# A Mamba and mixture-of-experts layer on one core: opening and first two units rewritten

## The reference, in short

```
dt = softplus(x_dbl[..., :R] @ dt_w.T + dt_b)
dA = exp(dt_t[..., None] * A);  h = h * dA + (dt_t * u_t)[..., None] * B_t[:, None, :]
y  = einsum('bdn,bn->bd', h, C_t) + u * Dp
```

## Time and profile before

| what | us |
|---|---|
| median of 3 runs | 554.12 (553.49 to 556.9) |
| profiled execution, its own time | 556.38 |
| its span, first to last instruction | 554.6 |

### The profile page before, as it was taken

One profiled execution on the slowest core, in us unless ns is written; L12 is line 12 of the kernel. 1 busy time (PEld: TensorE's weight loads), 2 busy tenths in 40 slices (PEclk: granted clock), 3 DMA queues, 4 the chain that ended last, 5 costly groups with the idle time before them and its releaser, 6 DMA issues.

```text
span 554.6 us, 5648 instructions
## 1 busy us (share of the span) xinstructions
PE 463.7 (84%) x1651; PEld 180.5 (33%) x1651; DVE 484.3 (87%) x599; ACT 375.3 (68%) x660; POOL 473.1 (85%) x152
## 2 busy tenths in 40 slices
PE   2987886788979797979898898978997996795987
PEld 1433322323323242424233433333333332232433
DVE  3576785989999899999999999999999999999951
ACT  1478385777777778785977588768776785474633
POOL 5352589898998989899999999999999999999810
PEclk9999797997989898999999899999898998696999
DMA  4158484726163451707172717171726271700000
GB/s 60 13 51 253 89 247 71 240 80 242 58 199 108 137 172 36 261 31 240 68 233 77 240 60 252 66 251 59 226 92 234 75 243 47 258 18 9 0 11 19
DMA packets 50401, 71.05 MB, mean 128 GB/s; under 512 B 15891, under 2 KB 16835, under 8 KB 50371
## 3 DMA queue, kind: packets, MB, share of 16 engines
q1 hardware_dynamic: 47378, 69.36, 38.0%
q0 software_dynamic: 1024, 1.05, 3.4%
q10 hardware_dynamic: 1968, 0.29, 0.3%
HBM read 60.19 MB, written 10.49 MB: 127 GB/s over the span
## 4 chain that ended last, share of the span: by engine, by line
PE 37%; DVE 28%; issue 14%; POOL 10%; ACT 8%; SPq 1%; DMA 1%; DVEq 0%; POOLq 0%; ACTq 0%
DVE st L1538 15%; POOL st L490 8%; DVE st L1523 6%; PE ps L626 6%; PE ps L713 3%; PE ps L688 3%; PE ps L725 3%; PE ps L601 2%; POOL st L481 2%; PE ps L807 2%; PE ps L823 2%; ACT ps L1089 2%; PE ps L653 2%; ACT L989 1%; PE ps L665 1%
## 5 line engine op out<-in xcount | busy, mean ns | idle before, releaser
L490 POOL TENSOR_TENSOR st<-st,repC 128x2048 f32<-128x2048 f32 x63 | 285.3, 4535 | 18.4 <-ACT carry L1095 13.5
L1538 DVE TENSOR_TENSOR_SCAN st<-ps,carry,st 128x512 f32<-128x512 f32 x192 | 234.8, 1267 | 4.8 <-ACT ps L1089 4.2
L1089 ACT ACTIVATE ps<-dtS,negA 128x512 f32<-128x512 f32 x256 | 170.9, 681 | 48.2 <-DVE st L1538 47.0
L481 POOL TENSOR_TENSOR st<-duS,repB 128x2048 f32<-128x2048 f32 x30 | 136.1, 4537 | 0.0
L1538 DVE TENSOR_TENSOR_SCAN st<-ps,zero,st 128x512 f32<-128x512 f32 x64 | 78.9, 1270 | 7.7 <-ACT ps L1089 7.4
L713 PE MATMUL ps<-st,fold 128*32 128x512 f32 x504 | 69.6, 625 | 15.2 <-POOL st L490 15.0
L1523 DVE TENSOR_TENSOR st<-duS,ps 128x2048 f32<-128x2048 f32 x33 | 75.0, 2272 | 3.4 <-PE ps L688 3.2
L626 PE MATMUL ps<-act,wT 128*128 128x512 f32 x128 | 57.8, 594 | 0.3 <-ACT act L1032 0.3
L462 POOL DMA_INDIRECT x<-in_L_tok_ple_table,idx x32 | 30.5, 952 | 31.9 <-DMA dtS<-dt_dram 13.1
L688 PE MATMUL ps<-xr,Bw 128*128 128x512 f32 x68 | 39.2, 660 | 10.7 <-ACT bc_sb L1081 6.0
L665 PE MATMUL ps<-xr,wT 128*32 128x512 f32 x32 | 20.5, 726 | 21.7 <-DVE st L1523 21.7
(11 more groups left out here) (143 smaller groups left out, 636.4 us busy)
## 6 DMA issues: line engine op xcount, KB each, us to landing
dtS<-dt_dram SPq DMA_DIRECT2D x64, 256.0 KB, 4.3
duS<-du_dram SPq DMA_DIRECT2D x64, 256.0 KB, 3.5
repC<-bc_dram SPq DMA_DIRECT2D x64, 256.0 KB, 5.0
repB<-bc_dram SPq DMA_DIRECT2D x30, 256.0 KB, 3.1
dt_dram<-dt SPq DMA_DIRECT2D x16, 256.0 KB, 3.1
du_dram<-du SPq DMA_DIRECT2D x16, 256.0 KB, 2.0
bc_dram<-bc_sb SPq DMA_DIRECT2D x16, 64.0 KB, 4.9
out_h<-fin SPq DMA_DIRECT2D x8, 128.0 KB, 2.0
```

The costliest lines, as they stand in the source:

```text
L481: pool.tensor_tensor(st[:, r], duS[:, u % 2], row, ALU.mult).then_inc(sem("dbu_pool"), 1)
L490: pool.tensor_tensor(st[:, r], st[:, r], row, ALU.mult).then_inc(sem("hc_ready"), 1)
L1089: sc.activation(decay_bank(u, r, q), dtS[:, u % 2, q], ACT.Exp, scale=negA[:, way(u), q, r:r + 1]).then_inc(sem("decay_ready"), 1)
L1538: dve.tensor_tensor_scan(st[:, r, q, order], decay_bank(u, r, q)[:, order], st[:, r, q, order], first, ALU.mult, ALU.add).then_inc(sem("sc ...
```

## The change

- Loads: the D vectors and the A logs (10 small loads) leave the per-direction lists and go last on SP, with a semaphore of their own, `rest_in`; both directions' `out_w` go into the second list. The conv taps count their own semaphore steps, and the scaled D matrices are made later (`skips`).
- Unit 0's dt and du are spread straight from SBUF; their stores to DRAM go, and the counts of `dt_in_dram` and `du_in_dram` drop by one store. `dt_out(1)` and `dt_times_x(1)` wait for the quarters instead.
- GpSimd issues its gathers 0 to 7, the mask and iota, then gathers 8 to 31, without the four waits.
- TensorE begins with matmuls of zeros and has a new order through unit 0; two PSUM banks are used otherwise (`BC_BANKS`: unit 0's B and C in bank 2; `b_bank`: row set 1 of unit 0 in bank Y).
- ScalarE and VectorE have a new order through the opening. Squares 1 to 3 move to VectorE (`norm_square`); unit 0's softplus is split differently: relu on VectorE, abs, exp, +1 (into `ga`) and ln on ScalarE (`first_abs`, `first_plus1`, `first_ln`).
- In unit 1 the softplus of unit 3 moves from position 0 to positions 3 to 10, `log1p_error(3)` to position 7, and unit 4's conv silu to the burst's end.
- The late weights are issued after unit 1's part of SP's loop.

```diff
+for dst, src in rest_loads:
+    sp.dma_start(dst, src).then_inc(sem("rest_in"), 16)
...
-sp.wait_ge(sem("dt_in_dram"), 16)
-spread(dtS[:, 0, q, :], dt_dram[0][rows]).then_inc(sem(f"dt_first_{q}"), 16)
-sp.wait_ge(sem("du_in_dram"), 16)
-spread(duS[:, 0, q, :], du_dram[0][rows]).then_inc(sem(f"du_first_{q}"), 16)
+sp.wait_ge(sem("dt_ready"), 1)
+spread(dtS[:, 0, q, :], dt[rows]).then_inc(sem(f"dt_first_{q}"), 16)
+sp.wait_ge(sem("du_ready"), 1)
+spread(duS[:, 0, q, :], du[rows]).then_inc(sem(f"du_first_{q}"), 16)
...
 store_bc(0)
-store_dt(0)
-store_du(0)
 for q in range(NQ):
     first_quarter(q)
 load_C(0)
...
     store_du(u + 2)
     load_du(u + 2)
     load_dt(u + 2)
+if u == 1:
+    with nc.allow_non_contiguous_dma(reason="b1 is 2 KB"):
+        for dst, src in late_loads:
+            sp.dma_start(dst, src).then_inc(sem("late_in"), 16)
...
-for t in range(TC, 2 * TC):
-    gather(t)
-pool.wait_ge(sem("uT_ready"), 2)
-for t in range(2 * TC, 3 * TC):
-    gather(t)
-pool.wait_ge(sem("act_ready"), 1)
-for t in range(3 * TC, TB):
-    gather(t)
-pool.wait_ge(sem("x_ready"), 1)
-for t in range(TB, TB + 4):
+for t in range(2 * TC, TILES):
     gather(t)
 for u in range(UNITS):
     if u:
         by_c(u - 1, NR - 1)
-    if u == 1:
-        dt_times_x(2)
     if u == 0:
-        pool.wait_ge(sem(f"dt_first_{NQ - 1}"), 16)
-        for t in range(TB + 4, TB + 12):
-            gather(t)
         dt_times_x(1)
     if 2 in on_pool(u):
         input_product(u, 2)
+    if u == 1:
+        dt_times_x(2)
     by_c(u, 0)
     by_c(u, 1)
     if u + 1 < UNITS:
         input_product(u + 1, 0)
     by_c(u, 2)
-    if u == 0:
-        for t in range(TB + 12, TILES):
-            gather(t)
     if 0 < u < UNITS - 2:
...
+pe.wait_ge(sem("idx_ready"), 1)
+pe.wait_ge(sem("pads_ready"), 1)
+write_nought(2, LONG)
 pe.wait_ge(sem("taps_ready"), 1)
 for s in range(2):
     turn(0, P * s, flat(taps[:, s]))
 turn(0, 2 * P, in_w[:, 1])
 turn(0, 3 * P, router_w).then_inc(sem("wT_ps"), 1)
-pe.wait_ge(sem("taps_ready"), 2)
+write_nought(1, LONG)
+pe.wait_ge(sem("taps_ready"), 5)
 for k in range(4):
     mm = turn(1, P * k, dir_taps[:, 0, k])
 mm.then_inc(sem("wT_ps"), 1)
...
 else:
+    pe.wait_ge(sem("dtproj_ready"), 2)
+pe.matmul(ps[0:2 * NS, BC_BANKS.get(u, SHORT), :], wT[:, 15, 2 * NS * way(u):2 * NS * way(u) + 2 * NS], x_of(u),
...
-    pe.wait_ge(sem("wT_late"), 1)
+    pe.wait_ge(sem("dbu_dve"), dve_nth[0, 1])
+    pe.wait_ge(sem("skips_ready"), 2)
 pe.matmul(ps[:, Y, :], skip[:, way(u), :], x_of(u), start=True, stop=False, skip_group_check=True)
...
+write_nought(1, LONG)
 dt_weights(0, 7)
 way_b_weights()
-write_nought(1, 0)
+write_nought(1, LONG)
 turn_chunk(0)
+write_nought(1, 1)
+x_chunk(0, 1)
+gate_chunk(0, 0)
+turn_chunk(1)
+conv(0, 1)
+x_chunk(1, 0)
+pre(0)
 dt_weights(1, 9)
-write_nought(1, 0)
-x_chunk(0, 1)
-write_nought(1, 0)
-conv(0, 1)
-pre(0)
 bc(0)
-write_nought(2, 0)
-turn_chunk(1)
-gate_chunk(0, 0)
+conv(1, 1)
 b_rows(0, 0)
-x_chunk(1, 1)
-turn_chunk(2)
-conv(1, 2)
 pre(1)
 bc(1)
-skip_product(0)
-add_nought(3)
+write_nought(2, Y)
+turn_chunk(2)
+write_nought(2, Y)
 turn_chunk(3)
 b_rows(0, 1)
 sum_dt(1)
+b_rows(0, 2)
 x_chunk(2, LONG)
-b_rows(0, 2)
 x_chunk(3, ZED)
+skip_product(0)
+add_nought(1)
 conv(2, PRE)
 b_rows(0, 3)
 sum_states(0, 0)
 zed(0, ZED, 0)
 conv(3, LONG)
 pre(2)
+bc(2)
 sum_states(0, 1)
-bc(2)
 b_rows(1, 1)
+add_nought(2)
 sum_dt(2)
 for u in range(1, UNITS):
...
     bc(u + 2)
-if u + 2 < UNITS:
+if u == 1:
+    pre(3)
+if u > 1 and u + 2 < UNITS:
     sum_dt(u + 2)
 if is_unit(u - 1):
...
 if is_unit(u - 1):
     partial(u - 1)
+if u == 1:
+    sum_dt(3)
 if third:
...
 def dt_out(u):
     sc.wait_ge(sem("dt_ps"), u)
-    wait(sc, "dt_in_dram", 16 * u)
+    if u == 1:
+        for q in range(NQ):
+            sc.wait_ge(sem(f"dt_first_{q}"), 16)
+    else:
+        sc.wait_ge(sem("dt_in_dram"), 16 * (u - 1))
     sc.wait_ge(sem("du_ready"), u)
     sc.activation(dt[:], ps[:, PRE, :], ACT.Copy).then_inc(sem("dt_ready"), 1)
...
     act_silu(CB + u - 2, LONG)
-if u + 3 < UNITS:
+if 1 != u < UNITS - 3:
     conv_silu(u + 3, PRE)
 for v in zeds(u):
     z_silu(v, ZED)
         gate_silu((v + 1) // 2 if u == 1 else 3, LONG)
     elif u == 1:
         gate_silu(2, LONG)
+if u == 1:
+    conv_silu(4, PRE)
 if 2 <= u <= CB + 1:
...
+def second_unit(p):
+    if p == 3:
+        dt_out(2)
+    if p == 4:
+        softplus_in(3)
+    if p == 5:
+        softplus_exp(3)
+    if p == 6:
+        softplus_plus1(3)
+        softplus_ln(3)
+    if p == 10:
+        dt_out(3)
...
 sc.wait_ge(sem("dtproj_ps"), 1)
 out_of_psum(dtproj[:, 0, :], ps[:, PRE, 2 * P:3 * P], "dtproj_ready")
-decay_rates(0)
 sc.wait_ge(sem("wT_ps"), 6)
 out_of_psum(dt_wT[:, 1], ps[0:R, 2, P:2 * P])
 out_of_psum(wT[:, 15, 2 * NS:4 * NS], ps[:, 2, 0:2 * NS])
 uT_chunk(0)
+rsqrt(1)
 silu_tables()
 act_silu(0, 1)
+gate_silu(0, 0)
+uT_chunk(1)
+conv_silu(0, 1)
+act_silu(1, 0)
+exp_ln_tables()
+first_abs()
+softplus_exp(0)
+first_plus1()
+first_ln()
 sc.wait_ge(sem("dtproj_ps"), 2)
 out_of_psum(dtproj[:, 1, :], ps[:, 2, 2 * P:3 * P], "dtproj_ready")
-squares(1)
-conv_silu(0, 1)
+bc_out(0)
+silu_tables()
+conv_silu(1, 1)
 exp_ln_tables()
-squares(2)
-rsqrt(1)
-softplus_in(0)
-softplus_exp(0)
-softplus_plus1(0)
-softplus_ln(0)
+decay_rates(0)
+decay_rates(1)
 rsqrt(2)
-bc_out(0)
-decay_rates(1)
-uT_chunk(1)
-silu_tables()
-gate_silu(0, 0)
-act_silu(1, 1)
-uT_chunk(2)
-squares(3)
-conv_silu(1, 2)
-exp_ln_tables()
 rsqrt(3)
-sc.wait_ge(sem("rates_ready"), 1)
+sc.wait_ge(sem("rates_ready"), 2)
 def first_unit(p):
+    if p == 0:
+        bc_out(1)
+        softplus_in(1)
     if p == 1:
-        softplus_in(1)
-        bc_out(1)
+        uT_chunk(2)
+        softplus_exp(1)
     if p == 2:
-        softplus_exp(1)
         softplus_plus1(1)
+        softplus_ln(1)
     if p == 3:
-        softplus_ln(1)
         uT_chunk(3)
     if p == 5:
         keep_last(0, 0)
         z_silu(0, ZED)
         conv_silu(3, LONG)
         exp_ln_tables()
+    if p == 12:
+        bc_out(2)
+        softplus_in(2)
     if p == 13:
         keep_last(0, 2)
-        softplus_in(2)
+        softplus_exp(2)
     if p == 14:
-        softplus_exp(2)
         softplus_plus1(2)
-    if p == 15:
         softplus_ln(2)
-        bc_out(2)
...
+def norm_square(n):
+    dve.wait_ge(sem("centred"), n + 1)
+    wait(dve, "ln_var", n)
+    dve.tensor_tensor(sq[:], xc[:, n % 2], xc[:, n % 2], ALU.mult).then_inc(sem("squared"), 1)
...
-    log1p_error(0)
+def first_softplus_in():
+    dve.wait_ge(sem("pre_ps"), 1)
+    dve.tensor_scalar(v_[:], ps[:, PRE, :], dt_b[:, 0:1], 0.0, ALU.add, ALU.max) \
+       .then_inc(sem("sp_a"), 1)
+def first_softplus_out():
+    dve.wait_ge(sem("sp_e"), 1)
+    dve.tensor_tensor(v_[:], v_[:], e_[:], ALU.add).then_inc(sem("sp_ve"), 1)
+    dve.wait_ge(sem("sp_ve"), 1)
+    dve.wait_ge(sem("sp_w"), 1)
+    dve.scalar_tensor_tensor(e_[:], ga[:], -1.0, v_[:], ALU.add, ALU.subtract).then_inc(sem("sp_c"), 1)
     dve.wait_ge(sem("sp_c"), 1)
-    dve.tensor_tensor(l_[:], l_[:], e_[:], ALU.subtract).then_inc(sem("sp_log1p"), 1)
-    dve.wait_ge(sem("sp_log1p"), 1)
-    dve.tensor_tensor(dt[:], v_[:], l_[:], ALU.add).then_inc(sem("dt_ready"), 1)
+    dve.wait_ge(sem("sp_l"), 1)
+    dve.tensor_tensor(dt[:], l_[:], e_[:], ALU.subtract).then_inc(sem("dt_ready"), 1)
     dve.wait_ge(sem("dt_ready"), 1)
     dve.wait_ge(sem("x_ready"), 1)
...
 way_taps(0)
-pick_rates(0)
 way_taps(1)
-pick_rates(1)
 begin_norm(0)
 norm_var(0)
 norm_newton(0)
 start_u2(0)
 start_residual(0)
+begin_norm(1)
+norm_square(1)
+norm_var(1)
+norm_newton(1)
+start_u2(1)
 way_b_out()
 dve.wait_ge(sem("wT_copied"), 9)
 for d in range(2):
                             .unsqueeze(2).broadcast_to([P, NR, 32, 4])))
 ch.wait()
 dve.memset(zero[:], 0.0).then_inc(sem("rows_ready"), 1)
-rates(0)
-begin_norm(1)
-norm_var(1)
+start_residual(1)
 begin_norm(2)
+norm_square(2)
+norm_var(2)
+begin_norm(3)
+first_softplus_in()
+norm_square(3)
+first_softplus_out()
+norm_var(3)
+dve.wait_ge(sem("rest_in"), REST)
+pick_rates(0)
+pick_rates(1)
+skips()
 ch.mark(dve.tensor_scalar(minus[:], ident[:], -1.0, None, ALU.mult))
 ch.mark(dve.memset(xfT[DM:XR], 1.0))
 ch.mark(dve.memset(w1[XR - 1:XR], 0.0))
 ch.mark(dve.memset(router_wT[DM:DM + E, :], 0.0))
-norm_newton(1)
-start_u2(1)
-start_residual(1)
-norm_var(2)
-first_softplus()
-norm_newton(2)
-start_u2(2)
-start_residual(2)
-begin_norm(3)
-norm_var(3)
-rates(1)
 dve.wait_ge(sem("consts"), 1)
 ch.mark(dve.tensor_copy(rank[:], ranki[:]))
 ch.mark(dve.tensor_copy(w1[DM:DM + E], maskf))
+rates(0)
+rates(1)
+dve.wait_ge(sem("ln_log"), 4)
+norm_newton(2)
+start_u2(2)
 ch.wait()
 def input_product(u, r):
...
+if p == 7:
+    if u == 1:
+        log1p_error(3)
...
     start_u2(3)
 if p == 2:
+    start_residual(2)
+if p == 3:
     log1p_error(1)
+    input_product(0, 1)
     start_residual(3)
-if p == 3:
-    input_product(0, 1)
 if p == 5:
     input_product(0, 2)
```

99 lines of the change are left out of this document (55 added, 44 removed).

## The result

The changed kernel took **557.91 us** in the median of 20 runs (552.87 to 562.60), the kernel before 554.75 beside it (553.08 to 558.88, 20 runs): a ratio of **1.0042** (95% interval 1.0021 to 1.0062). That is a small loss, clear of no change, where a small gain was forecast (553.1). A ratio and its interval leave out executions more than 1.5% above the fastest of their kernel, which the medians count, so the two can differ a little. The profiled execution took 558.89, its span is 557.1.

The account below looks back on a forecast made before the run. VectorE bounds 122.5 to 260 us, GpSimd 260 to 480, both unchanged. First scan 4.4 us earlier, mostly given back in units 0 and 1, leaves -1.0: 553.1 us, own range 550 to 556.5, with rivals 546 to 560.

Parts of the forecast that it names:

- The opening: Stage before the first scan: reordered work makes du at 34.35 and starts the first scan at 45.1, 4.4 us earlier.
- The direct loads: Unit 0's dt and du spread from SBUF: costed at nothing, first quarters landing near 39.5 and 40.2, needed at 42.9.
- the cover named: Unit 1's conv chain ahead of the first scan, said to hide the loading of unit 0's dt and du.
- The price named for the case without the cover: At the first scan: at most the 2.4 us that it now waits past its product.
- the fourth case: Rival, chance 0.07: slow loads of unit 0's dt and du; half speed costs nothing, a third about 5 us, giving 558.
- Unit 0 and unit 1: Unit 0 takes 40.4 us and ends at 85.5, 1.55 earlier; unit 1 ends at 121.5, against 122.5.
- the named give-backs: In-order queues of units 0 and 1 that return most of the 4.4 us won at the first scan.
- The sum of -1.0: Total forecast change in us: unit 1's last scan ends at 121.5 in place of 122.5, carried to the kernel's end.
- The step that failed: Code after unit 1 is unchanged, so the change is worth what it moves unit 1's end, now at 122.5.
- Its warning: A shift of unit 1's end that doesn't reach the kernel's end would break the opening assumption; no size given.
- the gains of units 0 and 1 did not stay: Rival, chance 0.18, claimed they stay: 4.4 us of the first scan and 4.2 of unit 1 reach the end, 545.5.
- the first of them: Rival, chance 0.28: TensorE's clock stays low through the opening, first scan at 49.9, 4.8 later than forecast, 557.9 us.

Follow-up runs that it names:

- the unfitted trial of the kernel before: The kernel before with three more matmuls of zeros in each unit from unit 2 on: 559.16 us, ratio 1.0073.
- fitted filling with one moved conv: The changed kernel with unit 1's conv ahead of bc(0) and matmuls of zeros fitted to idle time in units 2 to 9: 551.62 us, repeated 551.57.

## Why the prediction was wrong, and where it was right

**The opening** was right in the main. The third matmul of zeros ran at the full rate; du was done at 36.15 (34.35 forecast), TensorE stood 3.75 us ahead of `bc(0)` (4.6 forecast) and made the conv partly at half rate behind it, 5.37 us (5.2 forecast); the first scan came at 46.09 (45.1). `bc(0)` itself took 1.02, not the 1.7 of the forecast. The clock was low once more from 18.74 to 22.15, which the forecast didn't have: the first x chunk took 3.00 there, and 1.99 in the trial without the first matmuls of zeros, whose du was done at 35.13. The first scan doesn't need those matmuls: without them it moves by 0.2 us, in a single run.

**The direct loads.** "I cost them at nothing" held for the sum, but not for the part: the cover named was the conv chain, and without the direct loads that chain ends earlier than the loads by 3.56 us. The price named for the case without the cover, at most 2.4 us, came at the first scan (48.33 for 46.09), but unit 1 then ended 4.6 later. In that single run the direct loads are what lets the opening's gain through. Their slowness, the fourth case, did not show: the first product of the changed kernel waits for none of them, though their landing took a median of 5.7 us, where the later ones from DRAM took 3.3 and 4.1; what made them slower no run shows.

**Unit 0 and unit 1** were right: 85.6 and 120.9 for 85.5 and 121.5, with the named give-backs in their places (`sum_dt(1)` behind 5.57 us, `bc_out(3)` ahead of scan 3). But the end of unit 1 before, 122.6, was the latest of five profiles of the kernel before and its late-unit variants: 122.6, 121.5, 121.0, 121.1, 121.1, mean 121.5. Nine profiles with the changed kernel's first two units have 120.4 to 122.2, mean 121.2. The sum of -1.0 against the profile shown was -1.6; between the means it is about **-0.3**, which these spreads don't tell from nothing.

**The step that failed** is the first one: "none of that code changes. So a change in the first two units is worth what it moves the end of unit 1". The end of unit 1 was moved forward by 1.6 us in the two profiles, by little or nothing in the means, and the kernel was slower by 2 to 3. The late units are not a fixed length. From unit 1's end to the last instruction it takes 432.0 and 430.2 us in the two profiles of the kernel before, and 436.1 and 436.3 in the changed kernel's. A shift does carry over where the low stretches fall the same: that length is 435.9 to 436.7 in four variants of the changed kernel (the late weights early, through DRAM, no first zeros, the conv moved without filling), whose unit 1 ends anywhere from 117.9 to 125.6. TensorE pauses in each late unit for VectorE and GpSimd, its clock falls near some of these pauses, and in units 7 to 9 a low stretch is on the path of GpSimd, the bound: 226.2 us from du to du without it, 229.8 with it. Both profiles of the changed kernel have it, neither of the kernel before. How often the other executions have it can be estimated by their clock: the eight profiles with it at its full length are at 0.918 to 0.926, the six others without filling in most units at 0.930 to 0.950. With 0.926 as the mark, 27 of the changed kernel's 32 executions have it, and 15 of the 143 of the kernel before. The prediction read the low clock in the opening and in two single gaps, asked of it only what it costs there, and had no rival in which a shift changes where it falls later. Its warning, that a shift of unit 1's end that doesn't reach the end of the kernel would break the first step, is what happened.

**The rivals** all fall: the clock was not low through the opening, the gains of units 0 and 1 did not stay, the loads did not hold the scans. That the time came close to the 557.9 of the first of them is chance: its first scan at 49.9 is not there.

What is open: by what path the distance goes from the first two units to units 4 and 6, since the code between is the same, and which distance decides. The distance of unit 4 alone doesn't. Filling the last units' pauses to fit was not tried; the unfitted trial of the kernel before lost its time there.

## What to carry to other kernels

A span of unchanged code is not a constant where TensorE's clock falls and rises in it: compare the same two marks (here du to du) in both traces before a shift ahead of it is carried to the end, and list the runs by their mean granted clock before a difference of half a per cent is laid to the change. Short pauses of TensorE ahead of a step on the path can be filled with matmuls of zeros, but only to the length of the pause: fitted filling with one moved conv gave the best version, 551.6 us, and unfitted filling cost the kernel before 4 us. A change that costs nothing by itself (the direct loads) can be what the others need; undo it alone to see it.

## What the hardware showed that was not expected

- A VectorE product of 128x512 with both operands in SBUF took 4.35 us while GpSimd's product ran (122.48 to 126.99), where du, a product of the same size and also of two SBUF operands, took 0.69 at 35.46 with no GpSimd product running. Twice the size took 4.87. GpSimd's next product took 4.97 behind the one and 5.50 behind the other, in place of 4.50. Two reductions with one operand took 0.72 together while GpSimd was busy. The Trainium skill (SBUF — State Buffer, "Who interferes with whom") says that a VectorE instruction with two SBUF inputs contends with a GpSimd instruction that reads SBUF, and that the later one waits until the first is done; the trace agrees, with an end at 127.54, 0.55 behind GpSimd's.
- The place of the low stretches repeats. The Trainium skill (TensorE: Matmul & The Clock Gate, "Part 1") says that the moment at which the clock rises under sustained matmuls varies from run to run. The falls late in this kernel repeat: the low stretch of unit 6 stood at the same distance from GpSimd's du product, to 0.08 us, in nine profiles of the changed kernel and its variants, whose unit 1 ended anywhere from 117.9 to 125.6 us.
- A kernel got faster by some 2.4 us with 0.72 us of useless work more on VectorE (a median of 555.88 against 558.3, though the intervals of the two ratios just overlap).
